# Cross attention of a two-layer decoder with the queries on partitions instead of the keys

## The reference, cut to what matters

```python
q = (x @ Wq).reshape(B, Nq, h, dh)            # 256 queries a batch
k = (context @ Wk).reshape(B, Nk, h, dh)      # 77 keys
v = (context @ Wv).reshape(B, Nk, h, dh)
scores = jnp.einsum('bqhd,bkhd->bhqk', q, k) * scale
attn = jax.nn.softmax(scores, axis=-1)
out = jnp.einsum('bhqk,bkhd->bqhd', attn, v).reshape(B, Nq, h * dh)
return out @ Wo + bo
...
x = _layernorm(x + _L0_xattn_ref(x, ctx_768, ...), axis=-1)
```

## Time and profile before

| What | Value |
|---|---|
| Time, median of 3 runs | 2533.46 us (2532.05 to 2538.2) |
| Time of the profiled execution | 2531.66 us |
| Its span, first to last instruction | 2529.9 us |
| TensorE busy | 1949.3 us, 77% of the span |
| VectorE, ScalarE, GpSimd busy | 1297.8, 943.5, 351.7 us |
| Mean granted clock of TensorE | 0.752 |
| First layer's mixer and cross attention | 0 to 717.6 us |
| Feed-forward block of the first layer | 717.6 to 1159 us |
| Second layer's self and cross attention | 1159 to 2098 us |

### The profile page before, as it was taken

The page is one execution under the profiler, slowest core; times in us unless marked ns, Lnnn a source line. Parts: engine busy times, 40 slices in busy tenths (PEclk is TensorE's granted clock), DMA queues, the critical chain, the costliest instruction groups (busy, mean ns, idle before and its releaser), DMA issues.

```text
span 2529.9 us, 36372 instructions
## 1 busy us (share of the span) xinstructions
PE 1949.3 (77%) x15584; PEld 1656.7 (65%) x15584; DVE 1297.8 (51%) x2486; ACT 943.5 (37%) x1100; POOL 351.7 (14%) x364
## 2 busy tenths in 40 slices
PE   5785985976979999996698679668856975666666
PEld 5575684775768888885567457556745664555555
DVE  3455454354445333335844574375548345667676
ACT  3233142333322333322623263153335232735535
POOL 1200000000023444432000200300030011000000
PEclk9678687688589999998667766766785685666655
DMA  3000000000030000000000000000000001001000
GB/s 150 1 1 1 1 2 1 1 1 1 1 150 13 26 26 26 13 1 1 1 1 9 18 1 1 26 1 1 2 25 1 1 26 50 26 1 43 1 9 10
DMA packets 8656, 42.21 MB, mean 17 GB/s; under 512 B 1072, under 2 KB 3376, under 8 KB 7472
## 3 DMA queue, kind: packets, MB, share of 16 engines
q1 hardware_dynamic: 8496, 39.89, 4.2%
HBM read 31.50 MB, written 8.39 MB: 16 GB/s over the span
## 4 chain that ended last, share of the span: by engine, by line
PE 56%; DVE 25%; ACT 12%; issue 4%; POOL 3%; DMA 1%; SPq 0%; POOLq 0%; DVEq 0%; ACTq 0%
PE ps L92 12%; PE ps L93 11%; PE ps L94 11%; DVE m L1345 9%; PE ps L626 5%; PE ps L547 5%; PE ps L607 4%; ACT r L1010 4%; DVE m L1356 4%; DVE sm L1356 3%; PE ps L663 3%; ACT m L1010 2%; DVE m L1353 2%; DVE r L1345 2%; POOL sm L1949 2%
## 5 line engine op out<-in xcount | busy, mean ns | idle before, releaser
L1010 ACT ACTIVATE r<-ps 128x1024 fp32r<-128x1024 f32 (+4 forms) x280 | 211.6, 788 | 808.9 <-PE ps L547 646.4
L1345 DVE TENSOR_TENSOR m<-m 128x1024 f16<-128x1024 f32 (+8 forms) x360 | 325.8, 928 | 206.1 <-ACT m L1095 71.7
L547 PE MATMUL ps<-cst,m 128*128 128x128 f32 (+1 forms) x1152 | 192.5, 341 | 96.7 <-DVE m L1753 28.4
L1345 DVE TENSOR_TENSOR r<-ps,r 128x1024 fp32r<-128x1024 f32 (+2 forms) x152 | 129.3, 868 | 253.0 <-ACT r L1010 252.9
L1840 POOL TENSOR_SCALAR sm<-sm 128x2 f32<-128x2 f32 x40 | 10.0, 250 | 1711.1 <-DVE sm L1372 1711.1
L547 PEld LDWEIGHTS ps<-cst,m 128*128 128x128 f32 (+1 forms) x1152 | 175.9, 184 | 107.7 <-DVE m L1345 31.0
L1345 DVE TENSOR_TENSOR m<-m,ps 128x1024 f32<-128x1024 f32 (+1 forms) x64 | 71.6, 1119 | 261.1 <-PE ps L94 185.3
L1356 DVE TENSOR_REDUCE m<-ps 128x4 f32<-128x1024 f32 (+1 forms) x144 | 155.0, 1142 | 23.3 <-PE ps L809 20.5
L851 PE MATMUL ps<-m 128*128 128x51 bf16 x1024 | 89.0, 205 | 92.1 <-DVE m L1345 89.7
L92 PE MATMUL ps<-r,w0h 128*128 128x256 f32 x448 | 134.3, 300 | 33.3 <-DVE r L1345 33.1
L1213 ACT ACTIVATE m<-ps,cst 128x1024 f16<-128x1024 f32 x128 | 152.4, 1191 | 8.5 <-PE ps L834 8.5
(11 more groups left out here) (193 smaller groups left out, 5042.5 us busy)
## 6 DMA issues: line engine op xcount, KB each, us to landing
raw<-wu_dram SPq DMA_DIRECT2D x12, 768.0 KB, 4.1
keep_dram<-m SPq DMA_DIRECT2D x8, 768.0 KB, 3.3
m<-keep_dram SPq DMA_DIRECT2D x8, 768.0 KB, 4.2
w1raw<-w_dram SPq DMA_DIRECT2D x1, 3840.0 KB, 14.4
w0raw<-w_dram SPq DMA_DIRECT2D x3, 1024.0 KB, 18.9
w1f<-w1f_dram SPq DMA_DIRECT2D x1, 2048.0 KB, 18.8
out_dram<-xres SPq DMA_DIRECT2D x16, 128.0 KB, 1.8
xres<-x_dram SPq DMA_DIRECT2D x1, 1536.0 KB, 13.3
```

Of the source, the lines that this page charges most:

```text
L547: return pe.transpose(o, i, ident[0:n, 0:n])
L1010: return act.activation(o, i, ACT.Copy)
L1345: return dve.tensor_tensor(o, a, b_, op)
```

## The change

The scores are formed once, with the queries on partitions. Softmax runs along the free side, and only then are the weights turned:

- Layout. `V` is one fp32 tile. `K` is block diagonal: head pair c has 154 columns, its even head in rows 0 to 63 and columns 0 to 76, its odd head in rows 64 to 127 and columns 77 to 153, with zeros elsewhere, which GpSimd writes ahead ("kz"). The scale of 0.125 is in the copy of K. The mixer's tiles in `m` are moved behind them, so `V` and `K` lie free while the mixer ends.
- Values and keys of a batch are projected before the wait for the mixer's layer norm (the last half of the keys waits only for its "add"). The keys take 98 columns instead of 78.
- Scores: for each unit `u` (eight heads i, 128 queries j) four fp32 matmuls of 128 rows, 128 weight columns and 154 columns.
- VectorE reduces the maxima of a unit, negated, into `mx[u]`. ScalarE takes one exponential a head (128x77) with the maximum as bias, and its accumulator gives the sum (`rc[u]`). VectorE takes the reciprocals, and GpSimd multiplies the unit by them.
- TensorE turns the weights: eight fp32 transposes a group of four heads; ScalarE copies them to `PT`.
- The values are weighed by one fp32 matmul a head (77 rows, 64 weight columns, 256 columns), even heads to partitions 0 to 63 and odd heads to 64 to 127. This is the layout that `wo` wants, so the 16 transposes at the end are gone; ScalarE and VectorE copy both parts out in four pieces.

```diff
 TensorE
-                pe.wait_ge(*(st.a_dve if L else st.l0_dve).at(b, "ln"))
-                turn_x(st, b, sig)
...
+                    values(v1_, 1)
+                    keys(k0_, 0)
+                    pe.wait_ge(*mix_dve.at(b, "add"))
+                    keys(k1_, 1)
+                yield
+                pe.wait_ge(*mix_dve.at(b, "ln"))
+                pe.wait_ge(*act_.at(b, "v0"))
+                turn_x(st, b, sig)
...
+                for u in range(4):
+                    i, j = u // 2, u % 2
+                    if u < 2:
+                        pe.wait_ge(*act_.at(b, f"q{u}"))
+                    else:
+                        pe.wait_ge(*act_.at(b, f"e{u - 2}"))
+                    for n in range(4):
+                        m = pe.matmul(bank(st, 2 * j + n // 2)[:, 154 * (n % 2):154 * (n % 2) + 154], v.QT[:, 4 * i + n, j * 128:(j + 1) * 128], v.K[:, 4 * i + n, :], start=True, stop=True)
+                    m.then_inc(sig.up(b, f"s{u}"), 1)
...
+                def turn_p(g):
+                    i, a = g // 2, 4 * (g % 2)
+                    for hh in range(4):
+                        for j in range(2):
+                            m = tp(st.ps[0:CK, 256 * hh + 128 * j:256 * hh + 128 * j + 128], v.Pf[2 * i + j][:, CK * (a + hh):CK * (a + hh + 1)])
+                    m.then_inc(sig.up(b, f"t{g}"), 1)
...
+                        r = 64 * (hh % 2)
+                        m = pe.matmul(bank(st, 2 + g % 2)[r:r + 64, 256 * (hh // 2):256 * (hh // 2) + 256], v.V[:, 64 * h:64 * h + 64], v.PT[g % 2][:, 256 * hh:256 * hh + 256], start=True, stop=True)
+                    m.then_inc(sig.up(b, f"o{g}"), 1)
+
+                for g in G4:
+                    if g == 0:
+                        pe.wait_ge(*st.x_pool[L].at(b, "p1"))
+                        pe.wait_ge(*act_.at(b, "e2"))
+                    elif g == 2:
+                        pe.wait_ge(*st.x_pool[L].at(b, "p3"))
                     if g:
+                        pe.wait_ge(*act_.at(b, f"t{g - 1}"))
+                    turn_p(g)
+                    if g:
...
                         weigh_values(g - 1)
                     yield
 ScalarE
+                for u in range(4):
+                    act.wait_ge(*dve_.at(b, f"m{u}"))
+                    for h in range(8):
+                        o = bank(st, 2 * (u % 2) + h // 4)[:, CK * (h % 4):CK * (h % 4) + CK]
+                        e = act.activation(v.Pf[u][:, CK * h:CK * h + CK], o, ACT.Exp, bias=v.mx[u][:, h:h + 1], accum_out=v.rc[u][:, h:h + 1])
+                    e.then_inc(sig.up(b, f"e{u}"), 1)
+                    if u % 2:
+                        yield
+                for g in range(5):
+                    if g < 4:
+                        act.wait_ge(*pe_.at(b, f"t{g}"))
...
+                        copy(v.PT[g % 2], st.ps[0:CK, 0:1024]).then_inc(sig.up(b, f"t{g}"), 1)
+                    if g:
+                        act.wait_ge(*pe_.at(b, f"o{g - 1}"))
+                        copy(v.OT[0][:, 2 * g - 2:2 * g], k2(bank(st, 2 + (g - 1) % 2))).then_inc(sig.up(b, f"o{g - 1}"), 1)
                     yield
 VectorE
+                def shift(u):
+                    dve.wait_ge(*pe_.at(b, f"s{u}"))
...
+                    reduce(mx, src, ALU.max, negate=True).then_inc(sig.up(b, f"m{u}"), 1)
+
+                def sums(u):
+                    dve.wait_ge(*act_.at(b, f"e{u}"))
+                    dve.reciprocal(v.rc[u], v.rc[u]).then_inc(sig.up(b, f"r{u}"), 1)
 GpSimd
+                    pool.memset(v.Kf, 0.0).then_inc(sig.up(b, "kz"), 1)
...
+                for u in range(4):
+                    pool.wait_ge(*st.x_dve[L].at(b, f"r{u}"))
+                    pw = v.Pf[u].rearrange("p (h n) -> p h n", h=8)
+                    pool.tensor_tensor(pw, pw, v.rc[u].unsqueeze(2).to_broadcast([P, 8, CK]), ALU.mult).then_inc(sig.up(b, f"p{u}"), 1)
```

More of the change, by code:

```diff
@@ L38 @@
 CP = 78
+CW = 98
 def places(lay):
@@ L621, in xattn @@
                     m.then_inc(sig.up(b, f"q{i}"), 1)
[L622 to L628, removed]
@@ L629, in xattn @@
-                pe.wait_ge(*dve_.at(b, "q1"))
-                values(1)
-                yield
[L632 to L638, removed]
-                        for hh in range(8):
-                            h = 8 * i + hh
-                            r = 64 * (h % 2)
-                            m = pe.matmul(bank(st, 2 * i + hh % 2)[:, CP * (hh // 2):CP * (hh // 2) + CP],
-                                          v.QT[0][r:r + 64, h // 2, j * 128:(j + 1) * 128], v.KT[0][r:r + 64, h // 2, :], start=True, stop=True)
-                        m.then_inc(sig.up(b, f"m{j}{i}"), 1)
-                    yield
@@ L1076, in xattn @@
                     act.wait_ge(*pe_.at(b, f"q{i}"))
-                    copy(v.QT[0][:, 4 * i:4 * i + 4], c4(pair(st, i))).then_inc(sig.up(b, f"q{i}"), 1)
-                    yield
-                act.wait_ge(*pe_.at(b, "k"))
-                for i in range(2):
-                    copy(v.KT[0][:, 4 * i:4 * i + 4], c4(bank(st, i)[:, 0:4 * CP])).then_inc(sig.up(b, f"k{i}"), 1)
-                values(1)
-                yield
-                yield
-                yield
-                act.wait_ge(*pe_.at(b, "nm"))
@@ L1097, in xattn @@
-                for g in G4:
-                    if L:
-                        exps(g)
-                    yield
-                    if not L:
-                        exps(g)
-                    yield
-                yield
-                for i in range(2):
-                    act.wait_ge(*pe_.at(b, f"oT{i}"))
-                    copy(v.QT[0][:, 4 * i:4 * i + 4], c4(pair(st, i))).then_inc(sig.up(b, f"oT{i}"), 1)
+                    copy(v.QT[:, 4 * i:4 * i + 4], c4(pair(st, i))).then_inc(sig.up(b, f"q{i}"), 1)
@@ L1116, in _ @@
             act.wait_ge(d_cst, 16)
-            copy(identr, ident).then_inc(identr_ok.up("identr"), 1)
             for name in ("win", "wxp", "wout"):
@@ L1854, in xattn @@
                 v, sig = x_views(st, L), st.x_pool[L]
-                pool.wait_ge(*(st.a_dve if L else st.l0_dve).at(b, "ln"))
-                if b >= 2:
-                    pool.wait_ge(*sig.at(b - 2, "rs"))
-                pool.memset(st.sm[:, 32:288], 0.0)
-                for i in range(3):
-                    t = pool.memset(v.V[i][:, :, 64:65], 0.0 if i else 1.0)
-                t.then_inc(sig.up(b, "one"), 1)
+                if L or b < 2:
+                    if L:
+                        pool.wait_ge(*st.a_dve.at(b, "oT"))
+                    pool.memset(v.Kf, 0.0).then_inc(sig.up(b, "kz"), 1)
+                yield
                 if L:
```

247 lines of the change are left out of this document (99 added, 148 removed).

## The result

The changed kernel takes 2546.2 us (median of 20 runs, 2527.4 to 2569.4); the kernel before 2533.1 (20 runs, 2522.1 to 2541.6). The ratio is 1.0038, with a 95% interval from 1.002 to 1.0057: slower by 0.4%, where 0.4% faster was forecast. The single times spread over 42 us, those of before over 19. The profiled execution took 2552.1 us, span 2550.3, so it lies 6 us above the median.

The account below looks back on a forecast made before the run. TensorE bounds the projections; an engine chain, mostly through TensorE, bounds the middle. Projections -2.6 and middle +1.3 give -1.3 us a pair, -10 over eight: 2531.66 becomes 2521.3, plus 1.8 for the median: 2523, range 2450 to 2610.

Parts of the forecast that it names:

- The first stream's values find the full clock; keys lose it ...; the second stream's values should win it back. I take 26: Projections: values and keys of a pair take 26 us, between 22 and 32; 20.6 at 2.4 GHz, 37.8 at 1.2.
- A pair's projections: Values, keys, turned x and queries sum to 41.6 us against 44.5 and 44.0; 2.6 saved a pair, between -3 and 6.
- I take 0.42: Exponentials on ScalarE: 0.42 us a head with accumulator, between 0.23 and 0.45, its read not overlapping; 64 take 26.9.
- Rival 2: Exponentials: accumulator nearly free at 0.25 us a head, scores become the limit; -12 us a pair at best; chance 15%.
- instead of 0.48: Scores on TensorE: an fp32 matmul of 154 columns takes 0.48 us at 2.4 GHz, 0.87 at 1.2.
- Turned weights and values: After the exponentials: remaining transposes 5.2 us, weighing two at once 10.1, low-clock start 2.4; 17.7 in all.
- rival 3: Clock stays low in turned weights and values: 29.1 us instead of 17.7, +91 in all, about 2614; chance 8%.
- TensorE comes out of its wait at 1.2 GHz, which costs 2.4: Start of turned weights, after waiting for the exponentials: the low clock adds 2.4 us, within the 17.7.
- The middle as a sum: Scores to weighed values: 31.0 + 17.7 = 48.7 us against 47.1 and 47.7; 1.3 longer a pair.
- rival 1: Weighing of values: column halves run in single file, +10.1 us a pair, +81 in all, about 2604; chance 26%.
- `y` follows at once: After the weighed values, `y` starts without delay and takes 11.5 us as before.
- GpSimd's products: GpSimd's product of 616 columns takes 1.5 us; the last is due some 6 us after it is ready, no wait allowed for.

Follow-up runs that it names:

- the clock held: Changed kernel plus fp32r matmuls with thrown-away results (40 and 10 a pair) around TensorE's wait for the exponentials; 2477.2 us.
- the late start: Changed kernel with TensorE waiting for the mixer's layer norm of a stream before that stream's values and keys; 2605.3 us.
- the old place: Changed kernel with the projections back in their earlier place and order, after the mixer's layer norm, keys still 98 columns; 2522.7 us.

## Why the prediction was wrong, by its own steps

**The step that failed: "The first stream's values find the full clock; keys lose it ...; the second stream's values should win it back. I take 26".** The first two parts were right from the second round on, though the keys lost the clock sooner, 2.3 to 4.9 us after they began. The third was not right: the second stream's values took 7.74 us, the price at 0.50, and its keys 10.84. Values and keys together were 31.3 us in this round, at the upper end of the bounds 22 to 32, and 36.9 in the first round, nearly the 37.8 worked out for the low clock throughout. A pair's projections were 46.8 to 47.0 in six rounds in place of 41.6, 45.5 in one and 56.4 in the first: 383.5 us instead of 333. The difference to before is +26.8 where -20.8 was forecast: 48 us, and this alone turned the sign. Shown by the run with the values first: the same instructions with the values ahead of all keys have projections of 42.3 us, close to the forecast, and the kernel is then 1.6% faster than before.

**Exponentials, over-priced.** "I take 0.42" a head; it is 0.30, since the read of the accumulator (0.19 long) overlaps with both neighbours, which the prediction ruled out, and adds 0.09 to the 0.21 of a bare exponential. 64 are 19.7 us, not 26.9. Rival 2's 0.25 a head comes from no row and no run: what the runs show is 0.30 with the accumulator and 0.21 without. Scores cost 0.27 us each instead of 0.48: the price had been taken from keys and values, and it does not carry over. With the values first, at the full clock, a key's records (98 columns, by turns 128 and 64 rows) start 0.20 us apart, a score's (154 columns, always 128 rows) 0.13. No run tests why. From the first score to the steady run of turned weights it is 23.0 us where 31.0 was forecast. That ScalarE sets the pace here was right: it is busy for 22.7 of them, and the run without the accumulator gives back 5.1 us a pair.

**Turned weights and values, and the clock in them.** At the full clock this stretch is 14.0 us, below the forecast 17.7 with its 2.4 for a low start (windows of the run with the clock held, then `y`):

```profile
328.20:342.20 14.00, 13.99 (x114) 9.28 (x113) 4.28 (x7) 11.17 (x14) 0.79 (x1) 1.00 0.00 1
342.20:353.50 11.30, 11.30 (x98) 11.30 (x96) 2.92 (x7) 0.60 (x1) 0.93 (x2) 1.00 0.00 1
```

In the changed kernel it is 21.1 in the second round and 26.4 where the clock never comes back, some 24 on average: near the middle between the forecast and rival 3 (29.1). "TensorE comes out of its wait at 1.2 GHz, which costs 2.4" was right in kind and wrong in size: behind the wait of 3.83 us the granted clock was 0.50, and it cost 9 to 10 us a pair, shown by holding the clock (middle 37.5 instead of 46.7). Rival 3 had 8%, and was half of what happened. The groups of eight transposes took 1.99 us at 0.50 and later in the same round 1.10 at 1.00, so here they ran at either clock.

**The middle as a sum.** Two errors went against each other: 8 too much for the exponentials, 6 too little for the clock. It came out 2 us a pair shorter than forecast, and 2.2 shorter than before, where 1.3 longer was forecast. The other 1.5 of that difference is the base: the prediction took the old middle from two rounds (47.1 and 47.7), and over all eight it is 48.9.

**Right.** The weighing of values two at once (rival 1 is out: 0.117 us a record against 0.227 by the whole array's price; that the two are the halves by columns is not shown). `y` follows at once. GpSimd's products were late for nothing: 1.22 us each, where 1.5 was taken. The projections fill the gap of some 2.4 us ahead of them.

**Why the range held.** By luck: the errors of +48 and -28 us partly cancelled. That the time lies 0.9% from the forecast is thus no proof of the steps. The prediction did give slower 44%, but almost all of it for rivals 1 and 3. Rival 1 is out and rival 3 came half true in a middle that still became shorter; the loss in the projections that made the kernel slower had no rival of its own.

**What stays open.** Why the second stream's values do not win the clock back, though a shorter piece of the same work did so in the second layer of the kernel before (the earlier trace rows shows it at the full price): the runs show that the order decides, not by what. And when the clock comes back in the middle. Rounds of one profile with the same instructions differ by up to 12 us in it (31.3 and 43.2 without the accumulator), and profiles of neighbouring kernels too; nothing in the rows ahead of it tells which it will be. That it is what spreads the single times is consistent with most runs (5 to 18 us of spread with the clock held; 22 to 68 without), but not with all: the late start spread over only 17 us without it. The runs are also few, 4 to 20 of a kernel, and were not followed one by one.

## What to carry to other kernels

Price every stretch of fp32 or small matmuls at both clocks and ask what TensorE did just before. Here a stretch behind the mixer's dense matmuls found the high clock, one behind a wait of 2.4 to 3.8 us the low one (though not every such wait of this kernel did that, see below); and the most expensive work, the values, was best put first, while the clock was still high. A wait on TensorE of 2.5 to 3.8 us cost its own length and then some 6 to 10 us in what followed, so filling it with matmuls whose result is thrown away can be a large gain (here 69 us, and with the values first and the sums on VectorE 5.7% below the kernel before). When two edits of one change pull in different directions, only the stage table shows it; a total within 0.4% of before hid +27 and -18 us.

## What the runs showed of the hardware

- The granted clock fell to 0.50 between 2.2 and 6.4 us after the start of the keys of 98 columns, in every round in which they began at 1.00 (2.2 in a round with the values first and the clock held, 6.4 in a round with the old place, there 0.2 us behind the last key), and it stayed there with fp32r queries between the keys (19 us at 0.50, TensorE busy all the time). Fp32 values of 512 columns kept 1.00 for 8.2 us, but 7.74 us of them did not win it back in the changed kernel's second stream. In the second layer of the kernel before it was back 3.4 us after its fall, with four records of values in that time; what makes the difference is open.
- Ahead of the projections and of the turned weights the granted clock was down behind waits of 2.4 us (the kernel before), 2.5, 2.9, 3.1 and 3.8 us, and still up behind one of 2.1 us in the first round of two runs (keys of 78 columns alone; values first, clock held, no accumulator). The length alone does not decide: in the kernel before, TensorE stood still for 2.44 us up to 1390.7, ahead of fp32r matmuls of 512 columns, and the clock was 1.00 for the 5.3 us behind it.
- An exponential of 77 columns with bias takes 0.21 us from start to start, with the accumulator output 0.30.
- Fp32 matmuls of 77 rows and 64 weight columns, written by turns to output partitions 0 to 63 and 64 to 127, run two records at once (0.117 us a record of 256 columns, where the scores' price of 0.88 ns a column gives 0.227), and an order of 0, 2, 1, 3 is as fast as 0, 1, 2, 3.
